# Gated cross-attention layer on one core: six denominator bursts a quad instead of eight, with a DMA that merges pair sums

## What is computed

```python
q, k, v = Wq @ layernorm(x) + bq, Wk @ ctx + bk, Wv @ ctx + bv
mask = target_mask[:, :, :, None] * source_mask[:, :, None, :]
dot = mask * (q^T k / sqrt(32)) - (1.0 - mask) * 1e6
amap = softmax(dot, axis=-1) * mask
x = x + tanh(g_xattn[0]) * (amap @ v)
x = x + tanh(g_ffn[0]) * ffn(layernorm(x), W2)     # FP8-rounded operands, 1024 x 1024 weight
```

## Time and profile before

| | us |
|---|---|
| median of 3 runs | 2503.13 (2500.36 to 2506.14) |
| profiled execution | 2498.55 |
| its span in the profile | 2496.9 |
| PE busy in the span | 2441.7 |
| mean granted TensorE clock | 0.996 of full speed |

### The profile page before, as it was taken

One profiled execution on the slowest core, in us unless ns is written; L12 is line 12 of the kernel. 1 busy time (PEld: TensorE's weight loads), 2 busy tenths in 40 slices (PEclk: granted clock), 3 DMA queues, 4 the chain that ended last, 5 costly groups with the idle time before them and its releaser, 6 DMA issues.

```text
span 2496.9 us, 40504 instructions
## 1 busy us (share of the span) xinstructions
PE 2441.7 (98%) x13116; PEld 1382.0 (55%) x13177; DVE 1960.7 (79%) x3259; ACT 1387.1 (56%) x2606; POOL 1643.2 (66%) x1259
## 2 busy tenths in 40 slices
PE   7999999999999999999999999999999999999997
PEld 5888888875444444444444444444444444444442
DVE  6677776687788888888888888888888888888885
ACT  3333333315666666666666666666666666666664
POOL 2443333426777777777777777777777777777775
PEclk9999999999999999999999999999999999999999
DMA  6766666664444444444444444444444444444411
GB/s 245 262 243 237 234 235 235 227 188 100 94 102 98 102 101 102 97 94 95 94 93 100 92 92 92 92 92 101 92 93 95 99 101 102 98 101 97 104 45 56
DMA packets 241807, 313.48 MB, mean 126 GB/s; under 512 B 75000, under 2 KB 142648, under 8 KB 241624
## 3 DMA queue, kind: packets, MB, share of 16 engines
q1 hardware_dynamic: 230776, 275.56, 44.0%
q10 hardware_dynamic: 10848, 35.66, 4.0%
HBM read 199.83 MB, written 101.38 MB: 121 GB/s over the span
## 4 chain that ended last, share of the span: by engine, by line
PE 94%; DVE 1%; DMA 1%; issue 1%; POOL 1%; ACT 1%; SPq 0%; POOLq 0%; ACTq 0%; DVEq 0%
PE bank L863 22%; PE bank L893 20%; PE bank L848 20%; PE bank L878 19%; PE bank L904 9%; PE bank L940 4%; PE bank L933 1%; POOL pair_sum L398 1%; DMA q_st<-qx_scr 0%; DMA w_nat<-in_L_xattn_Wk_dram 0%; DMA v_scr<-stage 0%; ACT probs L715 0%; DVE x_raw L1043 0%; PE bank L802 0%; PE bank L924 0%
## 5 line engine op out<-in xcount | busy, mean ns | idle before, releaser
L398 POOL TENSOR_TENSOR pair_sum<-probs 128x512 f32<-128x512 f32 x1020 | 1279.2, 1286 | 399.0 <-ACT probs L715 399.0
L1143 DVE TENSOR_REDUCE part_max<-bank 128x1 f32<-128x512 f32 x2048 | 1276.6, 682 | 242.7 <-PE bank L878 229.2
L715 ACT ACTIVATE probs<-bank 128x512 f32<-128x512 f32 x2048 | 1067.4, 604 | 601.7 <-PE bank L863 578.7
L863 PE MATMUL bank<-q_st,k_st 100*128 100x512 f32 x2048 | 866.3, 425 | 6.0 <-ACT probs L715 6.0
L878 PE MATMUL bank<-k_st,q_st 98*128 98x512 f32 x2048 | 817.4, 399 | 8.3 <-DVE part_max L1143 6.5
L863 PEld LDWEIGHTS bank<-q_st,k_st 100*128 100x128 f32 x2048 | 387.4, 190 | 410.3 <-issue 211.2
L893 PE MATMUL bank<-probs,v_t 128*32 128x512 f32 x4096 | 545.6, 605 | 0.0
L878 PEld LDWEIGHTS bank<-k_st,q_st 98*128 98x128 f32 x2048 | 388.7, 190 | 129.2 <-DVE part_max L1143 15.8
L389 POOL TENSOR_TENSOR stage_lo<-stage,stage_hi 128x512 fp32r<-128x512 f32 x128 | 186.6, 1483 | 137.7 <-ACT stage_hi L661 136.2
L904 PE MATMUL bank<-pair_sum,ones 128*32 128x512 f32 x2040 | 265.5, 592 | 0.0
L661 ACT ACTIVATE stage_hi<-stage 128x512 fp32r<-128x512 f32 x128 | 80.2, 633 | 205.1 <-DVE stage L1007 142.9
(11 more groups left out here) (112 smaller groups left out, 2007.3 us busy)
## 6 DMA issues: line engine op xcount, KB each, us to landing
k_st<-k_scr SPq DMA_DIRECT2D x96, 512.0 KB
q_st<-q_scr SPq DMA_DIRECT2D x192, 256.0 KB
c_raw<-in_ctx_dram ACTq DMA_DIRECT2D x32, 512.0 KB, 7.0
k_scr<-stage_hi SPq DMA_DIRECT2D x64, 256.0 KB, 2.5
k_scr<-stage_lo SPq DMA_DIRECT2D x64, 256.0 KB, 2.7
v_scr<-stage SPq DMA_DIRECT2D x64, 256.0 KB, 2.9
q_scr<-stage_hi SPq DMA_DIRECT2D x64, 256.0 KB, 2.4
q_scr<-stage_lo SPq DMA_DIRECT2D x64, 256.0 KB, 2.7
```

The lines of the kernel that those rows point to most:

```text
L398: nc.gpsimd.tensor_tensor(pair_sum[:, r % 2, h], probs[:, a, h], probs[:, a + 1, h], ALU.add).then_inc(pair_done, 1)
L715: nc.scalar.activation(probs[:, c % PR, h, :], s_bank_of(n, k)[:, :], ACT.Exp).then_inc(exp_done, 1)
L863: nc.tensor.matmul(s_bank_of(n, k)[:, :], k_st[p][0:KS, h, j * P:(j + 1) * P], q_st[p][0:KS, th, h, :], start=True, stop=True).then_inc(sc ...
L1143: nc.vector.tensor_reduce(part_max[:, th, sh, at:at + 1], x_bank_of(n, "tile", k)[:, :], AX, ALU.max).then_inc(max_done, 2)
```

## The change

It does this:

- POOL's pair sums go to four buffers. `sums[0]` and `sums[1]` are the old two; `sums[2]` and `sums[3]` are the staging tiles of the first part. After pair sums 1 and 5 POOL issues a DMA with accumulate (`merge`): `sums[1] += sums[0]`, 1 MB read into 1 MB. So pair sums 0 and 4 have no burst of their own: 6 bursts a quad, at slots 27, 35, 43, 59 and at 3 and 11 of the next period. The bursts at slots 19 and 51 are gone.
- FFN bursts go from slots 31 and 47 to 39 and 51; `invert` from slots 23 and 55 to 19 and 51; two FP8 steps from slot 19 to 27.
- The multiplication of the inverse by gate and mask leaves DVE. ACT multiplies mask by gate once a period (`mask_gates`, slot 46), and POOL multiplies (`mask_inverse`) between the second and third addition of pair sums 2 and 6.
- `weigh` is split: half 0 after r = 0, half 1 after r = 3.
- On SP, half 0 of q is loaded for quad n + 2 at about slot 32 of period n instead of with k; `spread_inv(n-1, 1)` now stands ahead of `set_max(n, 1)`; `spread_inv(n, 0)` and `store(n-2)` now stand ahead of `set_max(n+1, 0)`; `turn_y8` stands behind `set_max(n, 1)`.

```diff
-            F_JOBS = {23: "max1", 31: "ffn0", 47: "ffn1", 55: "max0"}
+            F_JOBS = {23: "max1", 39: "ffn0", 51: "ffn1", 55: "max0"}
+            DEN_AT = {27: 0, 35: 1, 43: 2, 59: 3}
+            DEN_AFTER = {3: 4, 11: 5}
+            NG = 6
+            SUM_OF_GROUP = (2, 1, 3, 6, 5, 7)
+            GROUP_OF_SUM = {1: 1, 2: 0, 3: 2, 5: 4, 6: 3, 7: 5}
+            MERGED = (0, 4)
...
+                    def wait_sum_free(n, r):
+
+                        m, was = (n, r - 4) if r >= 4 else (n - 1, r + 4)
+                        if m < 0:
+                            return
+                        if was in MERGED:
+                            pool.wait_ge(merged[was // 4], 16 * (m + 1))
+                        else:
+                            pool.wait_ge(den_done, NG * m + GROUP_OF_SUM[was] + 1)
+
+                    def mask_inverse(m, th):
+
+                        pool.wait_ge(inv_done, 2 * (2 * m + th) + 1)
+                        pool.wait_ge(gates_masked, m + 1)
+                        nc.gpsimd.tensor_tensor(inv_c[:, :], inv_c[:, :], gtm_c[:, th], ALU.mult).then_inc(inv_done, 1)
+
                     def add_pair(n, r):
                         a = 2 * r % PR
-                        if counted(SJ * n + r - 1):
-                            pool.wait_ge(den_done, SJ * n + r - 1)
+                        wait_sum_free(n, r)
                         for h in range(QH):
+                            if (r, h) == (2, 2) and ordinary(n - 1):
+                                mask_inverse(n - 1, 1)
+                            if (r, h) == (6, 2):
+                                mask_inverse(n, 0)
                             pool.wait_ge(exp_done, NSLOT * n + 2 * QH * r + QH + h + 1)
-                            nc.gpsimd.tensor_tensor(pair_sum[:, r % 2, h], probs[:, a, h], probs[:, a + 1, h],
+                            nc.gpsimd.tensor_tensor(sums[r % 4][:, h], probs[:, a, h], probs[:, a + 1, h],
                                                     ALU.add).then_inc(pair_done, 1)
...
+                    def merge(n, th):
+
+                        pool.wait_ge(pair_done, QH * (SJ * n + 4 * th + 2))
+                        pool.dma_start(sums[1], sums[0], accum_op=ALU.add).then_inc(merged[th], 16)
+
+                    def weigh(m, th):
+
+                        pool.wait_ge(o_copied, 2 * m + th + 1)
+                        pool.wait_ge(inv_spread[th], 16 * (m + 1))
+                        if th == 0:
+
+                            if m > 0:
+                                pool.wait_ge(norm_done, NORM_STEPS * (m - 1) + 13)
+                            done = half_weighed
...
                     def period(n, p):
                         if n > 0 and real(n + 1):
                             stack_k(n + 1, 1 - p)
-                            stack_q(n + 1, 1 - p)
+                            stack_q(n + 1, 1, 1 - p)
                         if ordinary(n - 1):
                             move_den(n - 1, 1)
                             load_res(n - 1, 1 - p)
+                        if ordinary(n - 1):
+                            move_inv(n - 1, 1)
+                            spread_inv(n - 1, 1)
+                        if real(n):
+                            set_max(n, 1, p)
                         if ordinary(n - 2):
                             turn_y8(n - 2)
-                        if ordinary(n - 1):
-                            move_inv(n - 1, 1)
-                        if real(n):
-                            set_max(n, 1, p)
-                        if ordinary(n - 1):
-                            spread_inv(n - 1, 1)
                         if real(n):
                             load_tm(n)
                         if real(n + 1):
                             load_v(n + 1, 1 - p)
+                        if real(n) and real(n + 2):
+                            stack_q(n + 2, 0, p)
                         if real(n):
                             move_den(n, 0)
+                            move_inv(n, 0)
+                            spread_inv(n, 0)
                         if ordinary(n - 2):
                             store(n - 2, p)
-                        if real(n):
-                            move_inv(n, 0)
                         if real(n + 1):
                             set_max(n + 1, 0, 1 - p)
-                        if real(n):
-                            spread_inv(n, 0)
...
+                    def mask_gates(m):
+
+                        act.wait_ge(tm_loaded, 16 * TH * (m + 1))
...
+                        nc.scalar.activation(gtm_c[:, :, :], tm_c[:, :, :], ACT.Copy, scale=g1[:, 0:1]).then_inc(gates_masked, 1)
...
-                    def denominators(m, r):
-                        th, i = r // 4, r % 4
+                    def denominators(m, g):
+                        th, i = g // 3, g % 3
+                        r = SUM_OF_GROUP[g]
                         if i == 0:
                             if counted(2 * m + th):
                                 pe.wait_ge(den_copied, 2 * m + th)
-                        pe.wait_ge(pair_done, QH * SJ * m + QH * (r + 1))
+                        if i == 1:
+                            pe.wait_ge(merged[th], 16 * (m + 1))
+                        else:
+                            pe.wait_ge(pair_done, QH * SJ * m + QH * (r + 1))
...
-                    NORM_AT_2 = {3: (11,), 11: (12,), 19: (13, 14)}
+                    NORM_AT_2 = {3: (11,), 11: (12,), 27: (13, 14)}
```

More of the change, by code:

```diff
@@ L176, in flamingo_gated_layer @@
         init_done = sem("init_done")
-        stacked = [sem(f"stacked{i}") for i in range(TH)]
+        k_stacked = sem("k_stacked")
+        q_stacked = [sem(f"q_stacked{i}") for i in range(TH)]
         v_loaded = [sem(f"v_loaded{i}") for i in range(2)]
@@ L187, in flamingo_gated_layer @@
         pair_done = sem("pair_done")
+        merged = [sem(f"merged{i}") for i in range(TH)]
         pv_done = sem("pv_done")
@@ L263, in flamingo_gated_layer @@
             v_t = [sb(f"v_t{i}", [P, SJ, P], F32, at) for i in range(2)]
+            sums = [pair_sum[:, 0], pair_sum[:, 1], stage[:, :, :], stage_hi[:, :, :].bitcast(F32)]
             s_bank, o_bank, d_bank, x_bank = bank[0:3], bank[3], bank[4], bank[5:8]
@@ L416, in period @@
                         for r in range(SJ):
+                            if n == 0 and r == 0:
+                                wait_stage_free()
                             if real(n) and (n, r) != (LAST, SJ - 1):
                                 add_pair(n, r)
+                            if real(n) and r % 4 == 1:
+                                merge(n, r // 4)
+                            if r == 0 and ordinary(n - 1):
+                                weigh(n - 1, 0)
                             if r == 3 and ordinary(n - 1):
-                                weigh(n - 1)
+                                weigh(n - 1, 1)
                                 add_residual(n - 1, 1 - p)
```

119 lines of the change are left out of this document (69 added, 50 removed).

## The result

The changed kernel takes 2936.93 us (median of 4 runs, 2928.09 to 2940.97), the kernel before 2504.38 (4 runs, 2500.36 to 2506.14). The ratio is 1.1725, 95% interval 1.1694 to 1.1756: 433 us slower. The prediction had the direction (2543 us, slower), and its range ended at 2602. The execution profiled took 2928.09 us, with a mean granted clock of 0.928, against 0.996.

A forecast was written before the change was run, and what follows sets the result against it. PE was taken to bound the kernel. New waits of 1.6 + 0.7 + 0.4 + 0.4 = 3.1 us, 31 times, add 96.1; less 56.3 for bursts gives +39.8 on 2503.1: 2543 us, range 2444 to 2602.

The forecast's parts named there:

- rival A: Slots 0 and 32: max rows land late behind the spread, PE waits; 2543 us, spanning 2497 to 2602; chance 0.62.
- B: Slots 0 and 32: max rows are not held up by the spread; 2447 us with no new waits; chance 0.21.
- The wait at slot 0: PE waits at slot 0 for max rows queued behind spread and store: 1.2 to 1.85 us, 1.6 taken.
- The spread 1.42 later as now: SP's queue before slot 0: the spread is issued 1.42 us after the write of the inverse, at 1335.0.
- merge traffic: Merges in flight when the inverse is written delay its chain: 0.4 us at each of two places, 3 the bound.
- 1341.5: Time on the old trace's clock when slot 0's max rows land, issued at about 1336.0; or 0.7 earlier.
- At slot 32 the step: PE waits at slot 32 for max rows behind the spread: 0.1 to 1.0 us, 0.7 taken.
- C: A merge blocks the DMA engines; the inverse's write lands 3 us late at both places: 2704 us; chance 0.07.
- The bursts' 56.3 us: Two of 8 denominator bursts a quad go, 64 x 0.88 us in 32 quads, off PE's path.
- DVE ... I take 0: Moving the inversion to slots 19 and 51 costs nothing; bounds 6.5 us gain, 10 us loss (0.3 x 31).
- it has about 4 us from issue to use: The small denominator transfer, needed by the inversion four slots earlier, has about 4 us before its use.
- D: POOL or DVE becomes the bound, or a merge is late for its burst: 2530 us; chance 0.10.

The follow-up runs named there:

- e1: Changed kernel with SP's old order of max rows ahead of the inverse's spread in both halves, and the store last; 2533.73 us.
- e9: Kernel before with only the inverse's spread moved ahead of the max rows in both halves, store in its old place; 2527.83 us.
- e3: Kernel before with only SP's new order: spread ahead of the max rows in both halves, store too at the period's end; 2682.71 us.
- e2: Changed kernel, SP's new order kept, without the two merges (pair sums 0 and 4 left out of the denominators); 151 us slower than e6.
- e6: Changed kernel with max rows ahead of the spread, store last, and no merges (pair sums 0 and 4 left out); 2505.99 us.
- e5: e1 with the bursts of slots 27 and 59 moved four slots later, to 31 and 63; 2540.06 us.
- e7: e5 with the inversion back at slots 23 and 55, POOL's product one addition later, two FP8 steps at 31 and 63; 2551.12 us.
- e4: Changed kernel with only the store moved behind the max rows at the period's end; 2900.96 us.

## Why the prediction was wrong in size

**The mechanism (rival A) was right.** "The two reordered transfers eat more than the two bursts give": the waits stand at slots 0 and 32, longer at 0, and e1 removes them by the old order alone. e9 refutes B: with nothing else changed, the rows land after 4.72 us instead of 2.35.

**The wait at slot 0 was mis-sized: 1.6 us predicted, 4.71 in the period shown, 5.4 in the median.** Three parts of the step failed. (1) "The spread 1.42 later as now": it was 3.50, 2.1 more, of which 0.4 stood in the term for merge traffic; the write itself went out 0.7 us earlier against PE's slot 0 than reckoned (6.79 before it instead of 6.09). (2) The landing "1341.5" of rows issued "at about 1336.0" is 5.5 us; it was 6.89, and 6.91 in e3 without any merge, because the store holds the rows for 2.2 us in the periods shown (3.0 in the median) and not for the 1.3 assumed. (3) I took 1.6, under my own upper end of 1.85. The parts sum to 1.85 + 2.08 - 0.70 + 1.39 + 0.11 (spread and rows are issued 1.11 apart, not 1.0) = 4.73. At slot 32 the step said 0.7, with the same write: 2.74 in the period shown. e2 gives the step's own size without merges: 3.0 us at slot 0, so it was too small there by nearly half even so, and 0.3 at slot 32, less than said.

**Merge traffic, "0.4 at each of the two places", was the worst term.** From e2 to after, the median waits grow by 2.4 us at slot 0 and 2.6 at slot 32. C was right in its mechanism: the write lands only when the merge is through (0.16 us behind it), 2.1 us late, where C said 3. I gave it 0.07 because small transfers had shared engines with large ones before without delay; but all of those were on one queue, or plain. No row of before has an accumulating transfer on a second queue, and this bound, "3 is the bound", should have gone into the forecast's own range with A, since the two add up rather than exclude each other: A and C are both waits on one chain (write, spread, rows). The size was also off: a merge lands after 7.0 us, not 5, so it is under way for the whole of the write. By the fit of the Trainium skill, "DMA: Bandwidth & Descriptors", section "Anatomy of one DMA", from which the prediction estimated 4.4 us, the merge would have been over even earlier; the measured 7.0 decides. e1, e2 and e6 show that 252 of 431 us need both.

**The clock was in no term.** Each wait of some microseconds was priced at its own length. The record shows 2.3 and 1.8 us more behind it, with a stretch at clock 0.50, and 130 us in PE's busy time. Neither C nor A had it; with what it costs here, (280 + 127) / 280 = 1.45 times the wait, C's 8.3 us would have been 12.0 a period, and its time an estimated 2503 + 373 - 56 = 2820 us.

**The bursts' 56.3 us were not to be had.** The bursts went (the groups of PE have 512 + 512 + 504 = 1528 instructions of L988, as expected), and 0.88 each is right, as slots 16 to 19 show (3.93 to 3.07). What failed is "DVE ... I take 0", with the bound "a loss of 0.3 x 31". In e1, 2.25 us a period come back, above all in slots 20 to 27 and 52 to 59, 70 us in all; 1.28 of them, 40 us, are there without any merge. The step priced the inversion's duration, and missed its input: "it has about 4 us from issue to use" would have been enough without merges (2.7 us), but merge traffic was priced only for the inverse, and with it the transfer takes 6.0. It also kept the old durations of small DVE instructions at places where POOL now works. Of D, the merge late for its burst did not happen, but its sign "PE waits for pair_sum" did, 38.1 us over the span. The prediction moved the burst of pair sum 2 to slot 27 without comparing the two times: by its own times the sum ends at 1358.06 + 5.01 + 0.22 = 1363.3, and the burst would start at 1363.73 - 0.88 = 1362.85.

**Smaller terms.** POOL's issue of a merge measures 0.88 us behind an idle 0.30, near the 1.0 taken. ACT's copy, q and the halves of `weigh` show in no wait of PE. The start cost 14 us, which was not considered at all: the two extra buffers belong to the first part.

What stays open: how the merge holds the other queue inside a DMA engine (only its outcome was measured); how the 1.28 us that are there without merges divide between DVE, POOL's contention and pair sums (e5 and e7 only showed that each fix moves the wait on); why the rows land late in e4; and the second limit of the start.

## What to carry to other kernels

On one DMA queue, the place of a 16 KB transfer that PE waits for is worth more than two matmul bursts: before moving a broadcast or a store ahead of it, count back from its reader, and add the delay of every transfer that runs on another queue at that moment, because such delays add up on one chain. In a kernel like this one, price a wait on PE of several microseconds at about half more than its length (127 on 280 us here, 65 on 118 in e3), since the clock falls behind it, and price a saving on PE only as far as the next engine has room at those very slots (DVE at 79% on average had none at slots 20 to 27). DVE steps that slow beside POOL (here 0.16 to 0.70 us, 0.69 to 1.69) keep their old duration only as long as POOL stays out of their slots. And when a burst moves to an earlier slot, compare the end of its input with that slot.

## What the runs showed of the hardware

- A 1 MB accumulating DMA within SBUF, issued by POOL: 0.88 us of issue after 0.30 us idle, 6.9 us at least and 7.0 in the median to land. An 8 KB write of SP issued 3.6 to 3.75 us after it takes 3.5 us instead of 1.4 and lands 0.16 us behind it, and a 256 KB broadcast issued with it 10.4 to 11 instead of 4.4 to 4.9. The Trainium skill, "DMA: Bandwidth & Descriptors", section "Queues, rings and completion order", lets an engine turn to another queue only after a packet of descriptors; the delays are of that kind, but no run here shows the turn itself.
- On one queue, a 16 KB transfer to 2 partitions lands 2.35 us after its issue ahead of the 256 KB broadcast, 4.72 behind it, and 7.74 behind broadcast and store (before, e9, e3; medians).
- PE's granted clock stayed near its upper level over waits of about 0.66 us (e9, 0.994) and fell to its lower level behind waits of 4.71 us (slot 0; 0.50 from 1518.5 to 1522) and 2.74 us (slot 32; 0.55 from 1553.3 to 1557), where score matmuls took 0.63 us instead of 0.40.
- Beside POOL's additions, two kinds of 128 x 16 DVE instructions took 0.70 to 1.07 us instead of 0.16 to 0.41, and 128 x 1024 ones 1.6 to 1.7 instead of 0.69.
